# Reordering the attention slots of a two-layer cross-attention kernel: scores ahead of the weighted sums, sums into x behind the next softmax

## The chip, the cores and the metric

The kernel runs on one core of a Trainium2 chip. The metric is the time of one execution on the device, in microseconds (us). A core has a matrix engine (TensorE, "PE" in the profile; its weight loads are shown apart as "PEld"), a vector engine (VectorE, "DVE"), a scalar engine (ScalarE, "ACT"), a general engine (GpSimd, "POOL") and a queue engine that issues most of the DMAs (SyncE, "SP"). Each runs its own instruction list in order. They meet through semaphores only: an instruction adds to a counter when it is done, another waits until the counter has reached a value. TensorE writes its results to PSUM, eight banks of 128 partitions by 512 floats.

## The reference

A block of 32 batches of 64 rows of width 256 (2048 tokens) goes through two cross-attention layers with a feed-forward part, and then through a second, smaller block. The change touches only the two cross-attention layers:

```
h  = layer_norm(x)                                   # 2048 x 256
q, k, v = h @ wq + bq, ctx @ wk + bk, ctx @ wv + bv  # 16 heads of 128
k, v = with one more key and value row (bias_k, bias_v) per head
x  = x + softmax(q k' / sqrt(128)) v @ wo + bo       # for both layers
x  = x + gelu(layer_norm(x) @ w_fc1 + b_fc1) @ w_fc2 + b_fc2
# then a resampler block with 16 heads of 16, a mask, rmsnorm and a feed-forward part
```

All of it is float32. Keys and queries of one batch are 64 long, with the extra key 65.

## The kernel before, in words

Tokens are worked on in four groups g of 512 (`GTOK`). Heads go in pairs: a layer has 8 pairs (`HP`), so a layer has 32 units of work and the two layers have 64 (`SLOTS`). Unit n is head pair n // 4 and token group n % 4. To keep float32 accuracy with the faster matmul form, every operand is split in a rounded high half (`..HI`) and the rest, the low half (`..LO`), and each product is made of three matmuls (`three`, lines 167 to 169).

The loop over slots is written once for each engine, and the order of the calls in it is the order of work on that engine. Slot n works on unit n and finishes unit n-1 (a software pipeline):

- TensorE: `keys(n)`, `queries(n)` (12 matmuls of 512 columns each), `values(n, 0)`, then `weighted(n-1)` (probabilities times values, 16 plain float32 passes of 128 columns), `values(n, 1)` (12 matmuls of 256 columns, as the first half), `scores(n)` (32 short passes that use 64 columns of the array), `output(n-1)` (24 matmuls of 256 columns). In the first slot of a pair `bias_sums(n)` stands ahead of the scores. Slots with `bias_turns` (29 to 32 and 61 to 63) transpose what the extra value row needs; slots with `norm_turn` (1, 2, 31 to 34 and 63) transpose normalised rows for the next layer.
- ScalarE copies each result from PSUM: `keys_out`, `queries_out`, `values_out(n, 0)`, `weighted_out(n-1)` (which writes the high half CHI of the weighted sums, line 647), `values_out(n, 1)`, and then `exponential(n)`.
- VectorE: `softmax(n-1)` (sum, reciprocal, product, eight 32-row transposes into PRT, line 759), layer-norm pieces, `weighted_rest(n-1)` (the low half CLO, line 766), in every fourth slot `round_set` (the high half of the next pair's weights, line 726), `shifted(n)` (maximum of the scores and subtraction, lines 777 and 780), and `settle(n-1)`, which adds output(n-1) from PSUM into X (line 789).
- GpSimd makes the low halves of the weights behind `round_set` (line 332) and those of the normalised rows (`norm_lo`, line 162).

What ties them around the change: `scores(n)` waits for both query copies and for `shifted(n-1)` (`sub_done`). `weighted(n-1)` waits for the transposed probabilities (`pt_out`) and for `settle(n-2)` (`x_settled`), because it writes the two PSUM banks, 3 and 4, in which output(n-2) stood. `output(n-1)` writes the same two banks and waits for both parts of CLO (`c_lo`, set by `weighted_rest(n-1)`). `queries(n)` waits for the low half of the normalised rows (`norm.lo`).

Of the kernel before, what the change touches and what calls it, by code (L numbers as in the profile page):

```python
# [13 lines left out]
B, S, D = 32, 64, 256  # L14
# [29 lines left out]
def program(nc, x, ctx_in, mask, wall, vech, vecm, b_fc2, qw, kw, vw, ow, out_b, w1, w2, b2, out):  # L44
    es = ExitStack()
    with es:
# [138 lines left out]
        with ExitStack() as ph:  # L185
# [96 lines left out]
            with nc.Block() as block:  # L282
# [97 lines left out]
                def _(e):  # L380
# [28 lines left out]
                    def values(n, j):  # L409
                        pair, a, g = unit(n)  # L410
                        into = PROJ[2 + j] if n else PROJ[j]
                        if n:
                            e.wait_ge(k_out, 2 * n + j + 1)
                        for p in range(2):
                            t = g * GT + 2 * j + p
                            for c in range(DC):
                                i = three(e, into[:, p * 256:(p + 1) * 256],
                                          SRC_HI[:, 0, c, t * P:(t + 1) * P], SRC_LO[:, 0, c, t * P:(t + 1) * P],
                                          WHI[a][:, 2, c, :], WLO[a][:, 2, c, :], c == 0, c == DC - 1)
                        i.then_inc(v_done, 1)  # L420
# [17 lines left out]
                    def bias_sums(n):  # L438
                        pair, a, g = unit(n)
                        e.wait_ge(e_made, 1)  # L440
                        if n == 0:
                            e.wait_ge(w_in[0], 16)
                            e.wait_ge(norm.scaled, DC)
                        else:
                            e.wait_ge(sub_done, n)
                        for c in range(DC):
                            for h in range(2):
                                i = e.matmul(logits[:, 1, 448 + 32 * c:480 + 32 * c],
                                             W[a][:, 3, h, c * P:(c + 1) * P], E[:, 2 * pair + h, :],
                                             start=(h == 0), stop=(h == 1))  # L450
                        i.then_inc(bw_done, 1)
# [12 lines left out]
                    def weighted(u):  # L464
                        e.wait_ge(v_out, 2 * u + 2)
                        e.wait_ge(pt_out, u + 1)
                        if u:
                            e.wait_ge(x_settled, 2 * u)
                        for h in range(2):
                            for p in range(GT):  # L470
                                i = e.matmul(bank[3 + h][:, p * P:(p + 1) * P],  # L471
                                             V[u % 2][:, p, h * K:(h + 1) * K],
                                             PRT[:, h * GT + p, :], start=True, stop=True)
                            i.then_inc(c_done, 1)
# [45 lines left out]
                    for n in range(1, SLOTS):  # L520
                        pair, a, g = unit(n)
                        bias, turned_before, turned_now = bias_at(n), apply_at(n - 1), apply_at(n)
                        if n < G:
                            e.wait_ge(ctx_lo, n + 1)
                        if g == 0:
                            e.wait_ge(w_split, pair + 1)
                        keys(n)
                        if turned_before is not None:
                            k, tg = turned_before
                            e.wait_ge(norm.scaled, (k * G + tg + 1) * DC)  # L530
                        if bias_at(n - 1) is not None:
                            L, bg = bias_at(n - 1)
                            e.wait_ge(ptb_out, L * G + bg + 1)
                            e.wait_ge(bw_out, L + 1)
                        e.wait_ge(norm.lo, (n // UNITS * G + min(n % UNITS, G - 1) + 1) * DC)
                        queries(n)
                        values(n, 0)
                        if bias is not None:
                            e.wait_ge(q_out, 2 * n + 2)
                            bias_turns(*bias, PROJ, n - 1)  # L540
                        weighted(n - 1)
                        values(n, 1)
                        if turned_now is not None:
                            e.wait_ge(q_out, 2 * n + 2)
                            if bias is not None:
                                L, bg = bias
                                e.wait_ge(ptb_out, L * G + bg + 1)
                                e.wait_ge(bw_out, L + 1)
                            norm_turn(e, norm, *turned_now, PROJ)
                        if g == 0:  # L550
                            bias_sums(n)
                        scores(n)
                        output(n - 1)

                    def up(q):
# [56 lines left out]
                def _(e):  # L612
# [31 lines left out]
                    def weighted_out(u):  # L644
                        for h in range(2):
                            e.wait_ge(c_done, 2 * u + 1 + h)
                            e.activation(CHI[:, h, :], bank[3 + h][:, :], ACT.Copy).then_inc(c_hi, 1)  # L647
# [21 lines left out]
                    for n in range(1, SLOTS):  # L669
                        bias, took, now = bias_at(n), stats_at(n), apply_at(n)  # L670
                        keys_out(n)
                        if n == 1:
                            ctx_round(3)
                        queries_out(n)
                        values_out(n, 0)
                        if bias is not None:
                            bias_out(*bias, PROJ[0])
                        weighted_out(n - 1)
                        values_out(n, 1)
                        if now is not None and now[0] == NL:  # L680
                            for c in range(DC):
                                scale_chunk(e, *now, c, PROJ)
                        elif now is not None:
                            scale_chunk(e, *now, 0, PROJ)
                        if took is not None:
                            norm_sqrt(e, norm, *took)
                        exponential(n)
                        if now is not None and now[0] < NL:
                            scale_chunk(e, *now, 1, PROJ)

# [30 lines left out]
                def _(e):  # L721
# [109 lines left out]
                    for n in range(1, SLOTS):  # L831
                        pair, a, g = unit(n)
                        bias, took, now = bias_at(n), stats_at(n), apply_at(n)
                        if g == 0:
                            e.wait_ge(exp_done, n)
                            bias_keys(n)
                        softmax(n - 1)
                        if n == 1:
                            ctx_rest(3)
                        if bias is not None and bias[1] == 0:  # L840
                            L, _ = bias
                            e.wait_ge(bw_turned, L + 1)
                            e.tensor_copy(BW[:, :], PROJ[1][0:32, 0:D]).then_inc(bw_out, 1)
                            if L + 1 < NL:
                                clear_sums(L + 1)
                        if now is not None:
                            norm_rstd(e, norm, *now)
                            norm_apply(e, norm, *now)
                        if took is not None:
                            k, tg = took  # L850
                            if k == 0:
                                e.wait_ge(x_in[tg], 16)
                            else:
                                e.wait_ge(x_settled, 2 * (n - 1))
                            norm_stats(e, norm, *took)
                        weighted_rest(n - 1)
                        if g == 2 and pair + 1 < NL * HP + 1:
                            round_set(pair + 1, 1 - a)
                        if n == SLOTS - 1:

                            e.wait_ge(w_in[1], 8 * SETS)
                            e.wait_ge(v_done, 2 * SLOTS)
                            e.tensor_copy(WHI[1][:, 0:3, :, :], W[1][:, 0:3, :, :]).then_inc(fc2_hi, 1)
                        shifted(n)
                        settle(n - 1)

                    def rounded(q):
                        e.wait_ge(g_full, q + 1)
# [10 lines left out]
                                            ALU.add).then_inc(y_added, 1)  # L879

                    softmax(SLOTS - 1)
                    norm_rstd(e, norm, NL, 1)
                    norm_apply(e, norm, NL, 1)
                    rounded(0)
# [650 lines left out]
```

## Time and profile before

| what | us |
|---|---|
| runs | 1444.49, 1446.86, 1447.26 (median 1446.86) |
| the profiled execution, own time | 1444.7 |
| its span, first to last instruction | 1442.9 |
| busy TensorE, weight loads, VectorE, ScalarE, GpSimd | 1383.0, 1248.0, 904.3, 630.3, 335.4 |
| slots 1 to 63, first key matmul to the end of the last output | 33.4 to 978.8 |
| VectorE: `round_set` one instruction, `settle` two, | 1.22, 2 x 0.69 |
| VectorE: layer-norm apply and statistics of a group | about 1.6 and 2.0 |
| VectorE: bias-sum addition (line 774) | 0.22 |
| ScalarE: exponential, a table load ahead of it where one is needed | 0.64, 1.28 |

How to read rows of a timeline: start in us from the span's start, duration, engine, line of the kernel, operation, what is written <- what is read, shapes, and how many instructions the row merges. In brackets, where there is something, stands how long the engine was idle before and what ended that. Matmuls are pipelined: the next one starts before the modelled end of the one before, so start times are to be compared, not ends.

### The profile page before, as it was taken

To read this page: it belongs to the slowest core of one execution; us is meant where nothing else is said; L and a number is where in the kernel's file an instruction comes from. 1 tells how busy PE (TensorE), PEld (TensorE's weight loads), DVE (VectorE), ACT (ScalarE), POOL (GpSimd) and SP (SyncE) were. 2 spreads that over 40 slices of the span, in tenths; PEclk is the share of its full clock that TensorE was granted. 3 is DMA by queue.
4 is the path that set the end of the run, shared out by engine and by line. 5 is a ranking of instruction groups with operands and counts; after the bars stand their busy time and mean duration, and the time that the engine had idled before them with its cause. 6 is when DMAs were issued, how large, how long until landed. Compare 5 with 4: busy or idle time off the path is not lost. (4 is left out here: it accounts for less than half of the span.)

```text
span 1442.9 us, 28206 instructions
## 1 busy us (share of the span) xinstructions
PE 1383.0 (96%) x11543; PEld 1248.0 (86%) x11543; DVE 904.3 (63%) x1874; ACT 630.3 (44%) x1054; POOL 335.4 (23%) x289
## 2 busy tenths in 40 slices
PE   5999999999999999999999999997998999997898
PEld 4899999999998888899999999986887988886787
DVE  4866666666666776757666666677423587776322
ACT  4633434343343664343434343445323256665521
POOL 2201011010010212101011011015852045555654
PEclk9999999999999999999999999999999999999999
DMA  4100010000000000000000000000000000002000
GB/s 153 59 30 1 30 30 1 30 2 30 30 2 30 1 30 4 28 30 1 30 30 1 30 2 30 30 23 0 1 1 8 1 2 0 0 0 63 5 30 29
DMA packets 27994, 30.29 MB, mean 21 GB/s; under 512 B 683, under 2 KB 26867, under 8 KB 27891
## 3 DMA queue, kind: packets, MB, share of 16 engines
q1 hardware_dynamic: 27666, 28.72, 6.2%
q8 instruction: 78, 1.28, 0.4%
q14 instruction: 24, 0.20, 0.0%
q10 hardware_dynamic: 226, 0.10, 0.0%
HBM read 26.72 MB, written 2.10 MB: 20 GB/s over the span
## 5 line engine op out<-in xcount | busy, mean ns | idle before, releaser
L332 POOL TENSOR_TENSOR WLO<-W,WHI 128x512 fp32r<-128x512 f32 x64 | 80.8, 1292 | 765.9 <-DVE WHI L726 765.9
L167 PE MATMUL bank<-SRC_HI,WHI 128*128 128x512 f32 x576 | 230.7, 401 | 11.2 <-issue 6.9
L169 PE MATMUL bank<-SRC_HI,WLO 128*128 128x512 f32 x576 | 229.6, 399 | 0.0
L168 PE MATMUL bank<-SRC_LO,WHI 128*128 128x512 f32 x576 | 229.6, 399 | 0.0
L759 DVE STREAM_TRANSPOSE PRT<-PR 32x256 f32<-32x256 f32 x512 | 223.3, 436 | 8.4
L766 DVE TENSOR_TENSOR CLO<-bank,CHI 128x512 fp32r<-128x512 f32 x128 | 87.9, 690 | 145.6 <-ACT CHI L647 145.6
L624 ACT ACTIVATE KT<-bank,PH 128x512 f32<-128x512 f32 x128 | 88.0, 689 | 186.1 <-PE bank L169 186.1
L167 PE MATMUL bank<-WHI,CHI 128*128 128x256 f32 x576 | 167.5, 291 | 0.0
L168 PE MATMUL bank<-WLO,CHI 128*128 128x256 f32 x576 | 161.5, 280 | 0.0
L169 PE MATMUL bank<-WHI,CLO 128*128 128x256 f32 x576 | 161.0, 280 | 0.0
L167 PE MATMUL bank<-WHI,SRC_HI 128*128 128x256 f32 x512 | 148.5, 290 | 0.0
L168 PE MATMUL bank<-WLO,SRC_HI 128*128 128x256 f32 x512 | 143.1, 280 | 0.0
L169 PE MATMUL bank<-WHI,SRC_LO 128*128 128x256 f32 x512 | 143.0, 279 | 0.0
L167 PEld LDWEIGHTS bank<-SRC_HI,WHI 128*128 128x128 f32 x576 | 109.6, 190 | 35.0 <-issue 12.8
L169 PEld LDWEIGHTS bank<-SRC_HI,WLO 128*128 128x128 f32 x576 | 109.4, 190 | 26.5
L789 DVE TENSOR_TENSOR X<-X,bank 128x512 f32<-128x512 f32 x128 | 88.0, 687 | 68.1 <-PE bank L169 67.5
L631 ACT ACTIVATE QT<-bank,PH 128x512 f32<-128x512 f32 x128 | 88.1, 689 | 93.6 <-PE bank L169 93.6
L471 PE MATMUL bank<-PRT,V 128*128 128x128 f32 x1024 | 126.1, 277 | 2.9 <-DVE PRT L759 2.8
L168 PEld LDWEIGHTS bank<-SRC_LO,WHI 128*128 128x128 f32 x576 | 109.6, 190 | 22.0
L471 PEld LDWEIGHTS bank<-PRT,V 128*128 128x128 f32 x1024 | 120.8, 193 | 3.4 <-issue 3.3
L636 ACT ACTIVATE V<-bank 128x512 f32<-128x512 f32 x128 | 76.5, 598 | 97.7 <-PE bank L169 97.7
L167 PEld LDWEIGHTS bank<-WHI,CHI 128*128 128x128 f32 x576 | 108.1, 188 | 7.2 <-issue 2.7
(189 smaller groups left out, 2878.7 us busy)
## 6 DMA issues: line engine op xcount, KB each, us to landing
W<-in_wall SPq DMA_DIRECT2D x17, 1024.0 KB, 5.5
W<-in_ctx SPq DMA_DIRECT2D x4, 512.0 KB, 7.1
X<-in_x SPq DMA_DIRECT2D x4, 512.0 KB, 8.6
mlp_w<-in_w SPq DMA_DIRECT2D x2, 1024.0 KB, 8.6
out<-X SPq DMA_DIRECT2D x4, 512.0 KB, 2.9
W<-in_wall SPq DMA_DIRECT2D x1, 512.0 KB, 7.2
W<-in_wall SPq DMA_DIRECT2D x2, 256.0 KB, 8.9
W<-in_qw SPq DMA_DIRECT2D x1, 256.0 KB, 2.8
```

The lines of the kernel that those rows point to most:

```text
L167: e.matmul(dst, a_hi, b_hi, start=start, stop=False, **kw)
L168: e.matmul(dst, a_hi, b_lo, start=False, stop=False, **kw)
L169: return e.matmul(dst, a_lo, b_hi, start=False, stop=stop, **kw)
L332: i = e.tensor_tensor(WLO[a][:, j, :, :], W[a][:, j, :, :], WHI[a][:, j, :, :].bitcast(F32), ALU.subtract)
L471: i = e.matmul(bank[3 + h][:, p * P:(p + 1) * P], V[u % 2][:, p, h * K:(h + 1) * K], PRT[:, h * GT + p, :], start=True, stop=True)
L624: e.activation(KT[:, h, :, 0:S], PROJ[2 + h][:, :].rearrange("p (q k) -> p q k", k=S), ACT.Identity, bias=PH[:, 1, 2 * pair + h:2 * pair + ...
L631: e.activation(QT[:, h, :], PROJ[h][:, :], ACT.Identity, bias=PH[:, 0, 2 * pair + h:2 * pair + h + 1]).then_inc(q_out, 1)
L636: e.activation(V[n % 2][:, 2 * j:2 * j + 2, :], (PROJ[2 + j] if n else PROJ[j])[:, :].rearrange("p (t n) -> p t n", n=256), ACT.Copy).then ...
L759: i = e.transpose(PRT[b * S + z:b * S + z + 32, :, b * S + y:b * S + y + 32], PR[b * S + y:b * S + y + 32, :, z:z + 32])
L766: e.tensor_tensor(CLO[:, h, :], bank[3 + h][:, :], CHI[:, h, :].bitcast(F32), ALU.subtract).then_inc(c_lo, 1)
L789: e.tensor_tensor(xs, xs, bank[3 + j][:, :].rearrange("p (t n) -> p t n", n=256), ALU.add).then_inc(x_settled, 1)
```

## The change

TensorE's slot becomes keys, queries, first half of the values, scores, weighted sums, second half of the values, output. ScalarE makes the exponential ahead of the second value copy, and the bias copy behind the weighted sums. VectorE makes `shifted(n)` ahead of `weighted_rest(n-1)`, `round_set` ahead of both, and `settle(n-2)` behind `softmax(n-1)`, where `settle(n-1)` closed the slot. What each of these does is as it was.

```diff
--- TensorE, slot n
                         queries(n)
                         values(n, 0)
+                        if g == 0:
+                            bias_sums(n)
+                        scores(n)
+                        weighted(n - 1)
                         if bias is not None:
                             e.wait_ge(q_out, 2 * n + 2)
                             bias_turns(*bias, PROJ, n - 1)
-                        weighted(n - 1)
                         values(n, 1)
                         if turned_now is not None:
...
                             norm_turn(e, norm, *turned_now, PROJ)
-                        if g == 0:
-                            bias_sums(n)
-                        scores(n)
                         output(n - 1)
--- ScalarE, slot n
                         values_out(n, 0)
+                        weighted_out(n - 1)
                         if bias is not None:
                             bias_out(*bias, PROJ[0])
-                        weighted_out(n - 1)
+                        exponential(n)
                         values_out(n, 1)
...
                             norm_sqrt(e, norm, *took)
-                        exponential(n)
--- VectorE, slot n
                         softmax(n - 1)
+                        if n >= 2:
+                            settle(n - 2)
...
-                        if bias is not None and bias[1] == 0:
-                            L, _ = bias
-                            e.wait_ge(bw_turned, L + 1)
-                            e.tensor_copy(BW[:, :], PROJ[1][0:32, 0:D]).then_inc(bw_out, 1)
-                            if L + 1 < NL:
-                                clear_sums(L + 1)
...
-                        weighted_rest(n - 1)
                         if g == 2 and pair + 1 < NL * HP + 1:
                             round_set(pair + 1, 1 - a)
+                        shifted(n)
+                        weighted_rest(n - 1)
+                        if bias is not None and bias[1] == 0:
+                            L, _ = bias
+                            e.wait_ge(bw_turned, L + 1)
+                            e.tensor_copy(BW[:, :], PROJ[1][0:32, 0:D]).then_inc(bw_out, 1)
+                            if L + 1 < NL:
+                                clear_sums(L + 1)
                         if n == SLOTS - 1:
...
-                        shifted(n)
-                        settle(n - 1)
--- VectorE, behind the loop
                     softmax(SLOTS - 1)
+                    settle(SLOTS - 2)
                     norm_rstd(e, norm, NL, 1)
```

## Rows read from the trace of the kernel before

**Rows 1.** Busy time by stretch: TensorE, weight loads, VectorE, ScalarE, GpSimd; clock; DMA share.
```profile
100.00:447.00 347.00, 347.00 (x2920) 316.70 (x2919) 230.78 (x450) 138.71 (x216) 30.37 (x24) 1.00 0.06 18
```

**Rows 2.** Timeline of TensorE's matmuls, an ordinary slot and its borders.
```profile
399.97 1.15 PE L434 MATMUL logits<-KT,QT 128*64 128x65 f32 x32
401.05 0.38 PE L167 MATMUL bank<-WHI,CHI 128*128 128x256 f32 x1
401.28 0.28 PE L168 MATMUL bank<-WLO,CHI 128*128 128x256 f32 x1
...
403.99 0.39 PE L167 MATMUL bank<-SRC_HI,WHI 128*128 128x512 f32 x1
...
410.99 1.95 PE L471 MATMUL bank<-PRT,V 128*128 128x128 f32 x16
412.69 0.36 PE L167 MATMUL bank<-WHI,SRC_HI 128*128 128x256 f32 x1
...
414.08 0.28 PE L169 MATMUL bank<-WHI,SRC_LO 128*128 128x256 f32 x1
414.29 1.15 PE L434 MATMUL logits<-KT,QT 128*64 128x65 f32 x32
...
418.30 0.39 PE L167 MATMUL bank<-SRC_HI,WHI 128*128 128x512 f32 x1
```

**Rows 3.** Timeline of the same slot, a weight load and ScalarE's second copy.
```profile
412.98 0.60 ACT L647 ACTIVATE CHI<-bank 128x512 fp32r<-128x512 f32 x1 [0.30 <-PE bank L471]
413.96 0.19 PEld L169 LDWEIGHTS bank<-WHI,SRC_LO 128*128 128x128 f32 x1
```

**Rows 4.** Timeline of VectorE, the end of the slot before and this one.
```profile
401.90 0.70 DVE L780 TENSOR_TENSOR sub<-logits,mx 128x520 f32<-128x520 f32 x1
...
404.79 0.69 DVE L746 TENSOR_REDUCE sm<-ex 128x8 f32<-128x520 f32 x1
...
406.55 3.59 DVE L759 STREAM_TRANSPOSE PRT<-PR 32x256 f32<-32x256 f32 x8
412.71 0.69 DVE L766 TENSOR_TENSOR CLO<-bank,CHI 128x512 fp32r<-128x512 f32 x1 [2.58 <-ACT CHI L647]
413.61 0.69 DVE L766 TENSOR_TENSOR CLO<-bank,CHI 128x512 fp32r<-128x512 f32 x1 [0.20 <-ACT CHI L647]
```

**Rows 5.** Timeline after the slots: matmuls behind 64-wide and 128-wide ones; a wait for VectorE.
```profile
1173.27 1.16 PE L1270 MATMUL bank<-KL,QE 128*128 128x128 f32 x8
...
1175.65 1.06 PE L1270 MATMUL bank<-KL,QE 128*128 128x128 f32 x8
...
1397.19 0.68 DVE L991 TENSOR_TENSOR X<-X,bank 128x512 f32 x1
...
1397.92 0.19 PEld L167 LDWEIGHTS bank<-mlp_whi,m1gh 128*128 128x128 f32 x1 [0.62 <-DVE X L991]
1397.92 0.39 PE L167 MATMUL bank<-mlp_whi,m1gh 128*128 128x256 f32 x1 [0.18 <-DVE X L991]
...
1398.14 0.28 PE L168 MATMUL bank<-mlp_wlo,m1gh 128*128 128x256 f32 x1
```

**Rows 6.** Waits of TensorE (total, times, longest); timeline at slot 35's queries.
```profile
PE bank L167 <- issue: 6.9, 4, 4.0
...
549.88 2.54 POOL L162 TENSOR_TENSOR SRC_LO<-HT,SRC_HI 128x512 fp32r<-128x512 f32 x2
...
552.52 0.47 PE L167 MATMUL bank<-SRC_HI,WHI 128*128 128x512 f32 x1 [1.04 <-issue]
```

**Rows 7.** Timeline of slot 31, the transposes of bias and of layer norm.
```profile
488.22 0.60 PE L456 MATMUL bank<-ident,PTB 128*32 128x128 f32 x4
...
491.87 1.03 PE L136 MATMUL bank<-ident,XN 128*128 128x128 f32 x8
```

**Rows 8.** Timeline of slot 1, VectorE's low halves and the first output matmul.
```profile
48.20 1.28 DVE L766 TENSOR_TENSOR CLO<-bank,CHI 128x512 fp32r<-128x512 f32 x2
...
50.43 0.38 PE L167 MATMUL bank<-WHI,CHI 128*128 128x256 f32 x1
```

## The prediction, made before the changed kernel was run

> **What bounds the kernel now.** I read the busy sums by stretch first, then the timeline of one slot engine by engine, then the view of waits. In a stretch of 347 us, 24 slots long, TensorE is busy for 347.00 us of 347.00 at the full clock, while VectorE has 230.78 and ScalarE 138.71 [rows 1]. An ordinary slot lasts 418.30 - 403.99 = 14.31 us [rows 2]. No wait ends late there: the softmax transposes end at 406.55 + 3.59 = 410.14 and the weighted sums that need them start at 410.99, 0.85 us later [rows 2, 4]. So the slots are TensorE's own time, and taking slack away from others gains nothing. Only four waits of TensorE's projection matmuls are seen in the slots region, 6.9 us, of which one (4.0 us, at 24.2 us) is ahead of slot 1 [rows 6].
>
> **What the change moves.** Nothing is computed more or less; no DMA, no instruction is added on any engine. I call the first matmul of the second value half v.
>
> *Matmul order.* Scores are 64 columns wide, all around them 128. Entering them costs 414.29 - 414.08 = 0.21 against a step of 0.12 between value matmuls; leaving them, 401.05 to the second output matmul 401.28 is 0.23 instead of 0.12 [rows 2]. Both borders remain: values to scores, scores to weighted sums. Does leaving cost less when plain float32 follows? After another 64-wide group the eight fp32 matmuls take 1.16 us, after a 128-wide one 1.06 [rows 5], so the same 0.1. I take 0 for the new order; were the exit free, it would give back 0.2 per slot; were it dearer, at most another 0.1. The Trainium skill, "TensorEngine Tiling (Array Packing)", section "Key Properties", says that a change of tiling mode, not of tile alone, drains TensorE. By it the number of borders counts, two before and two after, which also gives 0; the trace agrees with its 0.1 at either border.
>
> *The wait for the low half.* Output(n-1) needs CLO, the second half of which is made so: last weighted matmul, ScalarE copies CHI at 412.98 for 0.60, VectorE subtracts at 413.61 for 0.69, done at 414.30 = v + 1.61 (v = 412.69) [rows 2 to 4]. Before, the values (v to 414.08 + 0.12) and the scores (1.08) lay between, and output began at v + 2.68: 1.07 us of cover. After, only the values lie between: the last value matmul starts at v + 1.39 [rows 2]. In an unbroken stream the weights of the next matmul load while the present one starts: load 413.96 for the matmul at 414.08 [rows 3]. Output's first load would thus be due at v + 1.39, but CLO lands at v + 1.61, and TensorE answers VectorE 0.05 later (1397.19 + 0.68 = 1397.87, load at 1397.92) [rows 5]. So it loads at v + 1.66, and since its load is no longer hidden, its second matmul starts 0.22 later (1398.14) at v + 1.88, where the unbroken stream would have it at v + 1.39 + 0.12 + 0.12 = v + 1.63. **Loss: 0.25 to 0.27, I take 0.26 us a slot.**
>
> Is CLO itself later? Its engines are now shared differently. VectorE does max and shift of slot n's scores first: they end 401.90 + 0.70 = 402.60, 2.63 after the scores began (399.97) [rows 2, 4]. The weighted sums begin 1.08 after the scores; their first copy CHI ends in time for CLO 1.72 after that (412.71 - 410.99) plus the 0.1 of the border, so at 2.90. VectorE is free 0.27 earlier; with the bias-sum addition (about 0.1 more) still 0.15. The exponential on ScalarE stands behind both CHI copies. The rounding of the next weight set (1.22) now stands ahead of max and shift, but the softmax starts as soon as the previous CLO is done, about 11.6 us into the slot before, runs 5.35, then the two sums into X (1.4, moved behind it), and leaves VectorE free near 4 us into a slot whose scores come at 7; the softmax's 5.35 is 404.79 to 410.14 [rows 4], the other durations are in the table of the profile before. There is room for rounding (1.2) or, in the layer-norm slots, apply and statistics (3.6). The sums into X now stand ahead of the weighted sums' wait for them: near 4 us against 8.1, no cost.
>
> *How many slots pay.* Slots 1, 2, 31 to 34 and 63 have eight layer-norm transposes between values and output (row time 1.03, about 0.9 of it ahead of the next matmul), slots 29 to 32 and 61 to 63 bias transposes (0.60, from 488.22 to the next group about 0.4) [rows 7]; both cover 0.26. 63 - 11 = 52 slots are left: 52 x 0.26 = **+13.5 us**.
>
> *What comes back.* The queries of slots 3, 34 and 35 now wait for the normalised rows' low half. At slot 35: GpSimd splits weights until 549.88, then makes two low halves until 552.42, and the matmul starts at 552.52 [rows 6]. The idle figure is 1.04 there; with the modelled tail of 0.17 and the unhidden load it is 1.27. After the change the rounding stands at the front of VectorE's slot, so the split ends 5 us earlier, and ScalarE scales right after the transposes instead of behind the exponential: the low half would be done about 1 us into the next slot, and is wanted at 2.8. For slot 34, whose last half is scaled behind a square root and its table load even after the change, it comes near 2.6. The three idle figures sum to 6.9 - 4.0 = 2.9, with 3 x 0.24 for what each hides: **-3.6 us**; between 0 and -3.6.
>
> *Slot 1.* There VectorE is the late one: statistics until 48.20, then both CLO until 49.48; output starts at 50.43 [rows 8]. Max and shift (1.43) now go ahead: CLO until 50.91, output's weights at 50.96, first unhidden: **+0.6 us**.
>
> *The end.* The last softmax, weighted sums and output stand where they stood; softmax(63) is ready earlier, worth 0.2 at most. 0 taken.
>
> Sum: 13.5 - 3.6 + 0.6 = **+10.5 us**. On the profiled execution: 1444.7 + 10.5 = 1455.2, span 1442.9 + 10.5 = 1453.4. The median of the three runs is 2.2 above the profiled one, so on it 1446.86 + 10.5 = **1457**. About 0.2% (2.9 us) is what a measurement of this kernel can tell from no change.
>
> **Rivals.**
> *A, exit of the scores free towards float32.* Then 0.2 of the 0.26 comes back in each slot: 52 x 0.06 - 3.6 + 0.6 = 0, 1447. For it: values to weighted sums shows no border. Against: rows 5. 7%.
> *B, the load is not held.* If only the matmul waits and its weights get loaded ahead, the loss is v + 1.66 against v + 1.51: 0.15 x 52 = 7.8, less 3.0: 1452. Against: in rows 5 load and matmul start together at 1397.92. The Trainium skill speaks for it: "TensorE: Matmul & The Clock Gate", section "The mechanism", has TensorE pull weight loads ahead of matmuls in flight. The trace agrees with that only where nothing is waited for. 13%.
> *C, faster.* The low half arrives in time after all (say ScalarE's copy is triggered by modelled ends that come later than the real ones, so that all of v + 1.61 shrinks by 0.3): only the waits for the queries remain, -3.0 to -3.6, 1443. Against: start times of both copies are recorded, and VectorE took them 117 times from ScalarE alone. 8%.
> *D, dearer.* VectorE's max and shift, once put ahead of CLO, run over the 0.27 of room. From 0.2 more than that (the gap between the two CLO) each 0.1 adds 0.1 a slot; 0.15 too late adds 7.8: 1465. It needs them about 0.5 later than now after the scores' start; nothing shows that. 5%.
>
> **How the numbers follow.** Forecast 67%: 52 x (0.22 to 0.30) with 0 to -3.6 and the end's 0.5 gives 1454 to 1463. A is within 0.2%, C faster, B and D slower, with a few per cent of the forecast's low tail in "same". Faster 8%, same 9%, slower 83%. The range 1448 to 1464 leaves out C, most of A and the far part of D, and allows for the spread of 2.8 us of the runs shown.
>
> **What would show it.** An ordinary slot of 14.57 us instead of 14.31. In the waits, weight loads of line 167 released by CLO (line 766), some 52 times about 0.2 us (the load alone shows it: the matmul pipe's modelled end at v + 1.67 covers the wait). TensorE still 100% busy in the stretch of rows 1: busy is not fast. Weighted sums' 16 matmuls 0.1 longer, first output matmul 0.38 as now. Slots 3, 34, 35 without the three idle pieces. A slot of 14.31 or less makes A or C true; 14.46 is B; max ending over 2.9 after the scores' start is D. Wrong altogether is any new wait on softmax or on X ahead of the weighted sums.

## The result and the profile after

The changed kernel takes 1460.03 us (median of 4, 1458.33 to 1461.24), the kernel before in the same rounds 1446.27: 13.8 us more, ratio 1.010 with a 95% interval of 1.0083 to 1.0117. I had forecast 1457, 10.5 us more. The profiled execution has a span of 1456.6 us against 1442.9, 13.6 more.

The stretch that answers to [rows 1] shows TensorE as busy as before, at the full clock:

```profile
100.00:447.00 347.00, 346.74 (x2873) 311.68 (x2871) 220.53 (x436) 133.85 (x212) 29.99 (x24) 1.00 0.05 16
```

Here 2873 matmuls are done where 2920 were. The same slot borders as in [rows 2], now in the changed kernel's timeline of TensorE:

```profile
394.35 0.40 PE L167 MATMUL bank<-SRC_HI,WHI 128*128 128x512 f32 x1
...
401.25 0.28 PE L169 MATMUL bank<-WHI,SRC_LO 128*128 128x256 f32 x1
401.46 1.15 PE L434 MATMUL logits<-KT,QT 128*64 128x65 f32 x32
402.54 2.05 PE L471 MATMUL bank<-PRT,V 128*128 128x128 f32 x16
...
404.35 0.36 PE L167 MATMUL bank<-WHI,SRC_HI 128*128 128x256 f32 x1
...
406.00 0.39 PE L167 MATMUL bank<-WHI,CHI 128*128 128x256 f32 x1
...
408.94 0.39 PE L167 MATMUL bank<-SRC_HI,WHI 128*128 128x512 f32 x1
```

The slot lasts 408.94 - 394.35 = 14.59 us instead of 14.31. Entering the scores costs the same 0.21, and the weighted sums behind them last 0.10 longer than in [rows 2] (2.05 against 1.95): the exit of the 64-wide group moved with it, as forecast.

What is new is seen in the weight loads, with the two engines that feed them (timeline of the same slot, to be held against [rows 3, 4]):

```profile
403.39 0.70 DVE L780 TENSOR_TENSOR sub<-logits,mx 128x520 f32<-128x520 f32 x1
404.36 0.69 DVE L766 TENSOR_TENSOR CLO<-bank,CHI 128x512 fp32r<-128x512 f32 x1 [0.27 <-ACT CHI L647]
404.63 0.60 ACT L647 ACTIVATE CHI<-bank 128x512 fp32r<-128x512 f32 x1 [0.30 <-PE bank L471]
405.26 0.69 DVE L766 TENSOR_TENSOR CLO<-bank,CHI 128x512 fp32r<-128x512 f32 x1 [0.20 <-ACT CHI L647]
405.61 0.19 PEld L169 LDWEIGHTS bank<-WHI,SRC_LO 128*128 128x128 f32 x1
406.00 0.19 PEld L167 LDWEIGHTS bank<-WHI,CHI 128*128 128x128 f32 x1 [0.20 <-DVE CLO L766]
406.23 0.19 PEld L169 LDWEIGHTS bank<-WHI,CLO 128*128 128x128 f32 x1
```

VectorE is free at 404.09 and waits 0.27 for ScalarE's copy, so max and shift delay nothing. The second CLO ends at 405.95 and output's first load follows at 406.00. That is v + 1.65 with v = 404.35; the loads before it come every 0.12, and the next was due near 405.73. The view of waits (total, times, longest) has this line; in the kernel before, CLO held TensorE once, for the output of unit 63:

```profile
PEld bank L167 <- DVE CLO L766: 12.6, 53, 1.4
```

Slots 3 to 28 and 35 to 60 are 52, and slot 1 makes 53 with the longest wait, 1.4. For the matmuls the same view has slot 1's wait alone (1.2 us), since in the other 52 slots their modelled ends cover it: a reader who looks only at the matmul rows finds TensorE busy for 346.74 of 347 us.

From the starts of the first key matmul of each slot:

| slots | before, us each | after, us each | together |
|---|---|---|---|
| 4 to 28 and 36 to 60 | 14.31, with bias sums 15.14 | 14.56, 15.37 | +12.2 |
| 3, 35 | 15.61, 15.59 | 14.55, 14.56 | -2.1 |
| 34 | 16.21 | 16.33 | +0.1 |
| 2, 33 | 15.15, 15.16 | 15.11, 15.18 | 0.0 |
| 29 to 32, 61 to 63 | 16.82, 16.64, 17.55, 18.38, 16.82, 16.64, 17.55 | 17.03, 16.87, 17.69, 18.49, 17.06, 16.83, 18.00 | +1.6 |
| start to the end of slot 1 | 53.33 | 54.02 | +0.7 |
| behind slot 63 | 464.2 | 465.4 | +1.2 |

The rows add up to the 13.6 us of the profiled executions but for rounding. Slot 1 itself is 0.46 longer; the other 0.22 stand ahead of it, as it starts at 33.60 instead of 33.38.

### The profile page after: what moved, and what is told of

It reads as the page before. It is cut to its first block and busy times, and to the rows that moved or that the text cites. A ratio compares the mean times of both kernels' runs of the same rounds, so it can differ in the third digit from the quotient of the medians.

```text
span 1456.6 us, 28207 instructions
## 1 busy us (share of the span) xinstructions
PE 1401.5 (96%) x11543; PEld 1254.1 (86%) x11543; DVE 891.3 (61%) x1874; ACT 624.4 (43%) x1055; POOL 334.3 (23%) x289
## 3 DMA queue, kind: packets, MB, share of 16 engines
q8 instruction: 78, 1.28, 0.4%
## 5 line engine op out<-in xcount | busy, mean ns | idle before, releaser
L777 DVE TENSOR_REDUCE mx<-logits 128x8 f32<-128x520 f32 x64 | 44.7, 698 | 193.0 <-PE logits L434 192.7
L647 ACT ACTIVATE CHI<-bank 128x512 fp32r<-128x512 f32 x128 | 76.4, 597 | 133.1 <-PE bank L471 133.1
L471 PE MATMUL bank<-PRT,V 128*128 128x128 f32 x1024 | 132.8, 283 | 0.7 <-DVE PRT L759 0.7
L168 PEld LDWEIGHTS bank<-WLO,CHI 128*128 128x128 f32 x576 | 109.1, 189 | 0.7
```

The lines of the kernel that those rows point to most:

```text
L168: e.matmul(dst, a_hi, b_lo, start=False, stop=False, **kw)
L471: i = e.matmul(bank[3 + h][:, p * P:(p + 1) * P], V[u % 2][:, p, h * K:(h + 1) * K], PRT[:, h * GT + p, :], start=True, stop=True)
L777: e.tensor_reduce(mx[:, :].rearrange("p (h t) -> p h t", h=2), logit, AX_X, ALU.max).then_inc(mx_done, 1)
```

## The experiments

All but the last start from the changed kernel; "slot" without more is an ordinary one.

**1. Output waits for half of CLO.** Output's first three matmuls use head 0 alone, and write bank 3, which the second CLO does not read.

```diff
-                        e.wait_ge(c_lo, 2 * u + 2)
+                        e.wait_ge(c_lo, 2 * u + (1 if bias is None else 2))
...
                                 for h in range(2):
+                                    if bias is None and (j, p, h) == (0, 0, 1):
+                                        e.wait_ge(c_lo, 2 * u + 2)
                                     i = three(...)
```

> The changed kernel with one edit: in slots without bias turns, output(n-1) starts on the first half of CLO (head 0) and waits for the second half only ahead of its first head-1 matmul, three matmuls (0.35 us) later. My theory (the whole loss of an ordinary slot is output's wait for the second CLO, 0.25 us): the wait of 0.2 us on the weight loads is gone, ordinary slots go from 14.56 to 14.30 us, the kernel from 1460.0 to about 1447 (52 slots x 0.25). Rival A' (the loss is the new order of matmuls itself, its borders between 64-wide and 128-wide groups): slots stay at 14.5 or more, the time at 1458 to 1460. Rival B' (the loss is VectorE making CLO later): the first half of CLO is late too and a wait of about 0.1 stays, 1452.

Measured: 1442.69 us (median of 6), ratio to the kernel before 0.9977 (0.9962 to 0.9992). Slots last 14.28 us. Of the 53 waits of weight loads on CLO the 52 in ordinary slots are gone; what is left of that line is in slot 1. In the timeline, output's first load follows the one before it by the 0.11 of the stream and stands ahead of the end of the second CLO (412.56 + 0.69 = 413.25):

```profile
411.93 0.60 ACT L649 ACTIVATE CHI<-bank 128x512 fp32r<-128x512 f32 x1 [0.29 <-PE bank L471]
412.56 0.69 DVE L768 TENSOR_TENSOR CLO<-bank,CHI 128x512 fp32r<-128x512 f32 x1 [0.20 <-ACT CHI L649]
412.92 0.19 PEld L169 LDWEIGHTS bank<-WHI,SRC_LO 128*128 128x128 f32 x1
413.03 0.19 PEld L167 LDWEIGHTS bank<-WHI,CHI 128*128 128x128 f32 x1
```

The copies and CLO stand to each other as before the edit; only what waits for them changed. The rival "order and borders cost it" is out, and so is "CLO comes later". The time went 4 us below my figure. The profiled executions show 2.2 of them: the span is 15.2 us shorter than the changed kernel's, where I had 13, with 1.5 of the rest in the ordinary slots (14.28, not 14.30, and 14.56 before the edit) and 0.9 ahead of slot 1. The other 2 are the difference between the medians and the profiled executions, and no trace places them.

**2. Half of the cover taken away.** Six of the twelve matmuls of the second value half go ahead of the weighted sums; `values` gets a third argument, the parts of the half that it makes.

```diff
                         scores(n)
+                        values(n, 1, (0,))
                         weighted(n - 1)
...
-                        values(n, 1)
+                        values(n, 1, (1,))
```

> The changed kernel with six of the twelve matmuls of the second value half (0.70 us) moved ahead of the weighted sums, so that only 0.70 us of work lies between them and output instead of 1.41. No matmul more or less. My theory: each us of cover taken away comes back as wait, so ordinary slots last 14.56 + 0.70 = 15.26 us, slots with bias turns alone (29, 30, 61, 62) 0.5 more, those with layer-norm transposes 0 to 0.1 more: 1460 + 37 + 2 = about 1499 us. Rival A' (borders and order): slots stay at 14.6, 1460 us.

Measured, one execution: 1498.85 us. Slots last 15.26 us, forecast 15.26; those with bias turns alone 0.3 to 0.5 more, forecast 0.5. In those with layer-norm transposes I had 0 to 0.1 and was wrong: 31 and 32 grew by 0.3, 34 and 63 by 0.7. Now the wait is longer than the modelled tail and shows on the matmuls too (timeline, then the view of waits):

```profile
422.75 0.69 DVE L768 TENSOR_TENSOR CLO<-bank,CHI 128x512 fp32r<-128x512 f32 x1 [0.20 <-ACT CHI L649]
423.49 0.19 PEld L167 LDWEIGHTS bank<-WHI,CHI 128*128 128x128 f32 x1 [0.91 <-DVE CLO L768]
423.49 0.39 PE L167 MATMUL bank<-WHI,CHI 128*128 128x256 f32 x1 [0.71 <-DVE CLO L768]
```

```profile
PEld bank L167 <- DVE CLO L768: 51.0, 53, 3.6
PE bank L167 <- DVE CLO L768: 40.2, 53, 3.3
```

0.70 us of cover less gives 0.69 us more per slot. So the loss was taken away in experiment 1 and made larger here, each time through the wait for CLO alone.

**3. The sums into X put back.** `settle(n-1)` closes VectorE's slot again, `settle(n-2)` is taken from behind the softmax.

```diff
                         softmax(n - 1)
-                        if n >= 2:
-                            settle(n - 2)
...
+                        settle(n - 1)
```

> The changed kernel with the sums into X put back: settle(n-1) closes VectorE's slot as before the change, instead of settle(n-2) behind the softmax. My theory: in ordinary slots this part of the change neither costs nor gains, 14.56 us stays (the softmax ends near 6.4 us in the slot, the weighted sums want it at 8.1). In the four layer-norm slots 30 to 33, VectorE's apply, statistics or rounding now end after the scores and push max and shift and CLO back, 0.5 to 1.5 us each: total 1460 + 3, between 1460 and 1465. Rival (moving the sums into X is what costs, since the weighted sums wait for them): ordinary slots fall to 14.3, about 1447.

Measured, one execution: 1459.63 us, slots 14.58. The move of the sums neither costs nor gains. Slots 30 to 33 grew by 0.00 to 0.06 only: the 0.5 to 1.5 us that I gave them do not come. CLO is indeed later there, by 0.4 to 0.8 us counted from the slot's start, but it had that much room: in slot 32, where it is 0.8 later, it still ends 0.46 ahead of output's first load.

**4. Weighted sums ahead of the scores.** Scores and values both stand between CHI and output again, VectorE makes CLO ahead of max and shift.

```diff
+                        weighted(n - 1)
                         if g == 0:
                             bias_sums(n)
                         scores(n)
-                        weighted(n - 1)
...
-                        shifted(n)
                         weighted_rest(n - 1)
+                        shifted(n)
```

> The changed kernel with TensorE's order weighted sums, scores, second value half, output, and on VectorE CLO ahead of max and shift; all else as changed (exponential ahead of the second value copy, sums into X behind the softmax). My theory: scores (1.08) and values (1.41) both cover the way to CLO again, ordinary slots 14.31 us; the idle of the queries of slots 3 and 35 stays away (2.3 us against the kernel before), that of slot 34 stays: about 1444 to 1446 us. Rival A' (moving the exponential and the sums into X costs on its own): slots above 14.4.

Measured: 1445.43 us (median of 10), ratio 0.9997 (0.9987 to 1.0006): the same as before. Slots last 14.33. The earlier exponential and the moved sums cost nothing in ordinary slots. What came back in slots 3 and 35 (2.6 us) and 34 (0.4) is lost again up to the end of slot 2 (1.3 us), in slot 63 (0.3), in the other bias slots (0.8) and in the ordinary ones (0.4 in all 50).

**5. ScalarE's layer-norm work together.** With experiment 1's edit, both scale chunks stand ahead of the square root; in slot 63 the exponential stands behind all of them.

```diff
-                        exponential(n)
+                        last = now is not None and now[0] == NL
+                        if not last:
+                            exponential(n)
                         values_out(n, 1)
-                        if now is not None and now[0] == NL:
+                        if now is not None:
                             for c in range(DC):
                                 scale_chunk(e, *now, c, PROJ)
-                        elif now is not None:
-                            scale_chunk(e, *now, 0, PROJ)
                         if took is not None:
                             norm_sqrt(e, norm, *took)
-                        if now is not None and now[0] < NL:
-                            scale_chunk(e, *now, 1, PROJ)
+                        if last:
+                            exponential(n)
```

> The kernel with the divided wait for CLO, and ScalarE's layer-norm work put together: in slots with transposes both scale chunks come right behind the second value copy and the square root with its table load (1.28 + 0.21 us) behind them; in slot 63 the exponential follows those as it did in the kernel before. My theory of the one idle that I had forecast to vanish and that stayed (slot 34's queries, 1.05 us): the second scale chunk stood behind the exponential's table load and the square root's, and GpSimd's low half behind it ended at 542.48, the queries began at 542.59. Now it is 1.5 us earlier: slot 34 falls from 16.25 to about 15.2 us, slot 63 from 18.0 to 17.6, together 1.4 us less: 1442.7 - 1.4 = about 1441.3. Rival (the rows' low half waits for VectorE's earlier work or for GpSimd itself): slot 34 stays above 16.

Measured: 1442.29 us (median of 11), ratio 0.998 (0.9971 to 0.9989). Slot 34 lasts 15.19 us (16.25 in experiment 1), slot 63 17.69 (18.00): 1.4 us less in these two, as expected; in the total, 0.4 us less is not told apart. In the changed kernel GpSimd's second low half had been the last to come (its timeline, then TensorE's):

```profile
541.20 1.28 POOL L162 TENSOR_TENSOR SRC_LO<-HT,SRC_HI 128x512 fp32r<-128x512 f32 x1 [1.55 <-ACT SRC_HI L279]
```

```profile
542.59 0.47 PE L167 MATMUL bank<-SRC_HI,WHI 128*128 128x512 f32 x1 [0.89 <-issue]
```

With the edit GpSimd makes both halves in one piece, long before TensorE wants them, and slot 34's queries have no idle in front:

```profile
530.93 2.64 POOL L162 TENSOR_TENSOR SRC_LO<-HT,SRC_HI 128x512 fp32r<-128x512 f32 x2 [14.56 <-ACT SRC_HI L279]
```

**6. Bias matmuls with 128 rows.** With experiment 1's edit, PTT and BW get 96 zero rows.

```diff
-            BW = sb("BW", [32, D], scope=ph)
+            BW = sb("BW", [P, D], scope=ph)
...
-            PTT = sb("PTT", [32, 512], scope=ph)
+            PTT = sb("PTT", [P, 512], scope=ph)
...
+                    e.memset(PTT[:, :], 0.0).then_inc(zeros_set, 1)
+                    e.memset(BW[:, :], 0.0).then_inc(zeros_set, 1)
```

> The kernel with the divided wait for CLO, and the four small matmuls of the bias values (32 rows of weights) made with 128 rows, the 96 new ones zero; the same columns stream. It tests the border rule in the seven slots with bias turns, which lost 0.1 to 0.23 us each that I had not forecast. Theory: each change of the tile form costs about 0.1; the change put a border of its own between values and these matmuls, where the scores' exit was before. With 128 rows two borders go (into them and out of them): slots 29, 30, 61, 62 0.15 to 0.25 us shorter (17.02 to about 16.8, 16.87 to about 16.7), 31, 32, 63 the same. Rival (these slots lost because the bias turns or their copies moved): no slot changes by more than 0.05.

Measured, one execution: 1439.54 us. Slots 29, 30, 61, 62: 16.63, 16.41, 16.63, 16.40 us, which is 0.39 to 0.46 less, twice what I expected; 31 and 32 fell by as much, which I had not expected at all. The last value matmul, the bias matmuls and the first output matmul in the changed kernel, and then here:

```profile
465.47 0.28 PE L169 MATMUL bank<-WHI,SRC_LO 128*128 128x256 f32 x1
465.68 1.99 PE L485 MATMUL bank<-BW,PTT 32*128 32x256 f32 x8
467.59 0.38 PE L167 MATMUL bank<-WHI,CHI 128*128 128x256 f32 x1
467.82 0.28 PE L168 MATMUL bank<-WLO,CHI 128*128 128x256 f32 x1
```

```profile
457.73 0.28 PE L169 MATMUL bank<-WHI,SRC_LO 128*128 128x256 f32 x1
457.85 1.89 PE L487 MATMUL bank<-BW,PTT 128*128 128x256 f32 x8
459.39 0.47 PE L167 MATMUL bank<-WHI,CHI 128*128 128x256 f32 x1
459.69 0.28 PE L168 MATMUL bank<-WLO,CHI 128*128 128x256 f32 x1
```

Into the group: 0.21 against 0.12, the border. From its first matmul to output's second: 2.14 against 1.84, 0.30 more. All of that lies inside the group (1.91 against 1.54 up to output's first matmul); a border out of it does not show apart, for the next step is 0.23 against 0.30. The border into the group is confirmed. That the 32-row matmuls themselves are dearer is what the runs show and the border does not explain.

**7. All three edits.**

> All edits together: divided wait, scale chunks ahead of the square root, 128 rows for the bias matmuls. If the three effects add up: 1442.7 - 1.4 - 1.4 = about 1440 us, 0.3 to 0.4% under the kernel before. If full rows bring nothing: 1441.3.

Measured: 1440.95 us (median of 5), ratio 0.9962 (0.9948 to 0.9976). Slot 34 is 15.19 and slots 29 to 32 are as in experiment 6: there the effects add up. In slot 63 they do more than that: the rows took nothing in experiment 6 (18.00) and the exponential 0.31 in experiment 5 (17.69), both together 0.71 (17.29).

**8. The exponential put back** behind the second value copy and the square root.

```diff
-                        exponential(n)
                         values_out(n, 1)
...
                             norm_sqrt(e, norm, *took)
+                        exponential(n)
```

> The changed kernel with the exponential put back behind the second value copy and the square root, all else changed. It undoes ScalarE's part alone. My theory: neither cost nor gain in ordinary slots, the second CHI copy stands ahead of the exponential in both; 14.56 us stays, the softmax starts about 0.6 us later with more than 4 us to spare, total 1459 to 1461. Rival (the earlier exponential is in CLO's way through the shared engines): ordinary slots below 14.5.

Measured, one execution: 1461.28 us, slots 14.56. No effect there, as expected. Only slots 32 to 34 grew (by 0.41, 0.27 and 2.54 us) and 63 shrank by 0.32; slot 34 I had not expected to be touched. Two things make up its 2.54, read from the timeline of TensorE and from the busy time of a stretch (columns as in [rows 1]):

```profile
543.70 0.47 PE L167 MATMUL bank<-SRC_HI,WHI 128*128 128x512 f32 x1 [1.95 <-issue]
```

```profile
544.50:548.00 3.50, 3.50 (x10) 2.73 (x9) 3.39 (x9) 0.69 (x1) 0.00 (x0) 0.51 0.00 0
```

The exponential's table load now stands between the two scale chunks together with the square root's, so the queries begin 4.91 us into the slot instead of 3.86: 1.05 us of idle more. After that idle of 1.95 us TensorE's granted clock fell for about 3.6 us to 0.51, its lower level (1.2 of 2.4 GHz), and the same queries took 1.5 us longer. Behind the changed kernel's idle of 0.89 the clock stayed at 1.00. The same calls put together in another order (experiment 5) take slot 34 to 15.19.

**9. The old order with the small edits.** The kernel before; VectorE rounds weights ahead of CLO, both scale chunks stand ahead of square root and exponential, and the bias matmuls have 128 rows.

```diff
-                        weighted_rest(n - 1)
                         if g == 2 and pair + 1 < NL * HP + 1:
                             round_set(pair + 1, 1 - a)
+                        weighted_rest(n - 1)
```

> The kernel before, its order of matmuls kept (scores between the second value half and output), with three small edits: VectorE rounds the next weight set ahead of CLO, ScalarE makes both scale chunks ahead of square root and exponential, and the bias matmuls have 128 rows. It asks whether the new order of the scores itself brings anything, or only what came along with it. My theory: nothing. Slots 3, 34 and 35 lose their idle (1.3 + 1.0 + 1.3 us), the seven bias slots about 0.3 each: 5.7 us less, 1446.2 - 5.7 = about 1440.5, the same as the new order with all edits (1440.95). Rival (the earlier softmax and the sums into X behind it are worth something in the slots): this kernel stays over 1443.

Measured: 1440.78 us (median of 7), ratio 0.9969 (0.9957 to 0.998). Slots last 14.32, slots 3 and 35 14.31 and 14.32, slot 34 15.67, bias slots 0.2 less. That is 4.7 us less where I had 5.7: slot 34 gave back 0.5 of 1.0 and the bias slots 1.4 of 2.1. It is as fast as experiment 7: in the time of the kernel the new order of the scores brings nothing that can be told. In the slots of the profiled executions experiment 7 is 2.5 us shorter (1.7 in the ordinary ones, 14.28 against 14.32, and 0.5 in slot 34), and behind them 2.8 us longer. Whether the 1.7 belong to the order or to the finer wait stays open, as the old order with the finer wait was not run.

## Why the prediction was right, point by point

- *TensorE is the bound, slack elsewhere is worth nothing.* Shown: slots without the wait last 14.28 to 14.33 us in both orders (experiments 1, 4, 9), and undoing VectorE's or ScalarE's part alone changes no ordinary slot (3, 8).
- *Loss 0.26 us a slot from the wait for CLO.* Measured 14.56 against 14.31 or 14.32, 0.25; load at v + 1.65 where I had v + 1.66. Experiments 1 and 2 show it to be the cause, and its size follows the cover one to one.
- *52 slots pay.* Right (53 waits with slot 1). 12.2 us over 50 of them, 12.7 with slots 3 and 35, against 13.5.
- *Borders, 0 in the sum.* Right in ordinary slots. **Here a term was missed in the bias slots**: before, the scores' exit and the bias matmuls' entry were one border, after they are two. I had counted only the cover there. They cost 0.1 to 0.24 each, 1.3 us without the part of slot 63 that experiment 5 takes back. The rule that I had cited from the Trainium skill ("TensorEngine Tiling (Array Packing)", "Key Properties", a change of tiling mode drains TensorE) would have told it, had I counted the borders in those slots too. The traces agree: the loss goes away with the 32-row form: at 128 rows the bias slots of the new order (16.63, 16.41 in experiment 7) are no longer than those of the old (16.64, 16.46 in experiment 9), and the edit took 0.39 to 0.46 from them in the new order and 0.18 to 0.24 in the old.
- *Queries' idle, -3.6.* **The step that was mis-sized**: slots 3 and 35 gave 2.1 net of the new wait (2.7 in experiment 1), slot 34 gave nothing. I had its low half at 2.6 us into the slot, due at 2.8; it came at 542.48 - 538.73 = 3.75. I had left out that the earlier exponential brings its own table load (1.28 us) ahead of the value copy and the scale chunks, as the square root was used before it. By the start of that value copy, 12.73 us into slot 33 against 11.94 in experiment 8, this is 0.8 us of the 1.15; the rest was not followed. Experiment 5 leaves this load where it is and takes the square root's out from between the chunks, and the idle is gone: it shows that the chunks' lateness was the cause, and not which of the two loads.
- *Slot 1, +0.6.* 0.46 in slot 1, for the reason given: CLO waits for max and shift, and output's first load for CLO. The rest of the 0.7 at its end was there before it began.
- *The end, 0.* Slot 63 took 0.44 more, 0.31 of it from the exponential ahead of the scale chunks, which I had moved past without costing it. Behind slot 63 there were 1.2 us more. That stretch took 463.2 to 467.4 us in all kernels here, whose code there is the same but for one pair of sums into X, so 1.2 is not told from scatter.

From 10.5 to the 13.6 of the profiled executions (13.8 by the medians): the wait and the queries together came to 12.2 - 2.1 + 0.1 = 10.2 where I had 13.5 - 3.6 = 9.9. That this is so close is luck, as two errors nearly cancel: the wait cost 0.8 less than I had, and 1.1 less came back from the queries. The bias slots and slot 63 gave 1.6 that I had not counted, the stretch behind them 1.2, and the time up to the end of slot 1 0.1 more.

Rival A (free exit) is refuted by 2.05 against 1.95 us; B (load not held) by the load at 406.00 and 14.56 instead of 14.46; C by the wait itself; D by VectorE's 0.27 us of idle ahead of CLO.

## What to carry to other kernels

When work is moved out from between a producer and its consumer on a saturated engine, subtract it from the cover and compare what is left with the whole round trip, here copy, subtract and reload of weights: 1.65 us against 1.39. A cover that is short of the round trip by 0.26 us costs little in one slot and 1% of the kernel in 52, and it can hide from the view of busy time. Often the cheaper cure is a finer wait: letting output begin on the half that is ready gave back 0.28 us in each of 50 slots, 14 us, with one more wait. And the time of the kernel shows nothing for the new order itself: the old one with three small edits was as fast as the new one with all edits (experiments 9 and 7).

## What the runs showed of the hardware that I had not expected

- A held weight load does not show on the matmul: the load was 0.27 us late and the slot 0.25 longer, while the matmul rows showed no idle at all.
- Matmuls with 32 rows of weights are dearer than the same with 96 zero rows added: 1.91 us from the group's first to output's first against 1.54, beside 0.09 at the entry (experiment 6).
- TensorE idled for 1.95 us in slot 34 of experiment 8, and behind that its clock was at half for about 3.6 us: of the 2.54 us that the slot lost, 1.5 were the clock and not the idle.
- Nearly the same code behind the slots took 463.2 to 467.4 us from kernel to kernel. TensorE's granted clock is not full there; two stretches of experiment 7 (columns as in [rows 1]) have 0.97 and 0.94, a mixture of its two levels, 1.2 and 2.4 GHz, while in its slots 2 to 63 it stays at 1.00. That the clock makes the difference between kernels is not shown.

```profile
1200.00:1320.00 120.00, 115.35 (x1419) 103.28 (x1420) 86.76 (x217) 78.59 (x177) 62.63 (x72) 0.97 0.06 19
1320.00:1430.00 110.00, 99.38 (x603) 88.22 (x602) 37.78 (x61) 39.84 (x77) 64.72 (x45) 0.94 0.05 16
```
